# Low parts of two product tiles made by an accumulating DMA, in a cross-interaction tower kernel on one Trainium2 core

## The chip, the cores and the metric

The kernel runs on 1 of the 8 cores of a Trainium2 chip. The metric is the device time of one execution in microseconds (us). The engines are named as the profile does: PE (TensorE), PEld (its weight loads), DVE (VectorE), ACT (ScalarE), POOL (GpSimd) and SP (SyncE, which here only issues DMAs).

## What is computed

1024 rows of 32 table lookups (64 values each) give `e`, of shape (1024, 32, 64). Two interaction layers follow, then three small dense layers.

```python
def _cin_layer(h, h0, W, b):
    Wr = W.reshape(W.shape[0], h.shape[1], h0.shape[1])
    return jax.nn.relu(jnp.einsum('bhd,bmd,ohm->bod', h, h0, Wr) + b[None, :, None])
x1 = _cin_layer(e, e, W1, b1)              # W1: 128 x (32*32)
direct2 = _cin_layer(x1[:, :64], e, W2, b2)  # W2: 128 x (64*32)
z = jnp.sum(jnp.concatenate([x1[:, 64:], direct2], axis=1), axis=-1)
h = relu(concat([z, dense_ctx]) @ W_top1 + b_top1)
h = relu(h @ W_top2 + b_top2);  y = h @ W_top3
```

## The kernel before

The batch is cut into 128 chunks of 8 rows; 8 rows by 64 values are the 512 columns (`N`) of every matmul. A step of the pipeline is one chunk `c`; steps run in a loop unrolled six times, with the first six and the last eight written out. All engines run their own `step`, tied by semaphores that count chunks.

**Layer 1** of a chunk contracts products of `e` with itself. POOL forms four tiles of them (`prod1`, L258) from `near` and `h0`; a remainder of 32 rows (`rem_a` times `rem_b`, L245) is formed for two chunks at once, split into a high and a low part (ACT L618, L619; POOL L267), and contracted by one more matmul (L522). ACT turns the result into `x1` (L607), SP copies it to all partitions by DMA (`x1rep`, L311), and ACT moves that to PSUM (`x1p`, L638).

**Layer 2** contracts products of `x1` with `e`: 16 tiles of 128 x 512. DVE forms eight from `near` (`pnear`) and eight from `far` (`pfar`), both at L459. Twelve tiles (all of `pnear`, half of `pfar`) are split for fp32r: ACT rounds them to a high part `phi` (L655, L666), DVE subtracts to get the low part `plo` (L464), and PE does three fp32r matmuls on each (L527, L528 with `phi`, L533 with `plo`). The four tiles left stay fp32 (`whole`, L538); PE does each of these matmuls in two passes, so two entries stand in the trace for each.

The order in a step is written out for each engine:

- PE: high parts of `pnear` (16 matmuls), layer 1 of chunk c+2 (L521, L522), `whole`, low parts (12), high parts of `pfar` (8).
- DVE: `pnear`, `pfar`, low parts of `pnear` (L464, waits for `phi`), low parts of `pfar`.
- ACT: `x1` of chunk c+1, in even steps the remainder's high parts, `phi` of `pnear`, `x1p` of c+1, `phi` of `pfar`, sums of layer 2 of c-1 and of layer 1 of c+1 (L602, eight each).
- POOL: `prod1` of c+2; in odd steps `rem_prod`, in even steps the remainder's low part and the copy of indices (L232); two table gathers (L237), which end seven chunks before the end.
- SP: `x1rep` (waits for `x1`), in odd steps the remainder rows (L306), `near` and `h0` of c+3 (waits for `pnear`), `far` of c+2, in even steps the store of gathered rows (L318).

`prod1` is one buffer, so POOL waits before it for the layer-1 matmuls that read the last contents:

```python
                    pool.wait_ge(acc1_ready, c + 2)
```

Of the kernel before, what the change touches and what calls it, by code (L numbers as in the profile page):

```python
# [32 lines left out]

T_NEAR = A2 * K1
T_SPLIT = T_NEAR + K2
# [3 lines left out]
def build_dlrm(nc, a):  # L39
# [7 lines left out]
    with ctx:  # L47
# [23 lines left out]
        w2T = sb("w2T", [P, K2, O])  # L71
# [11 lines left out]
        prod1 = sb("prod1", [P, K1, N])  # L83
# [27 lines left out]
        w1wide = prod1[:, :, :].rearrange("o a n -> o (a n)")  # L111
# [4 lines left out]
        hid2 = [prod1[:, 2 * h:2 * h + 2, :] for h in range(2)]  # L116
# [38 lines left out]
        pfar_ready = sem("pfar_ready")  # L155
        hi_near_ready = sem("hi_near_ready")
# [64 lines left out]
        @block.gpsimd  # L221
        def _(pool):
            nc.gpsimd.memset(ident[:, :], 0.0).then_inc(ident_zero, 1)
            pool.wait_ge(ident_zero, 1)
            nc.gpsimd.affine_select(out=ident[:, :], in_=ident[:, :], compare_op=ALU.not_equal, fill=1.0,
                                    base=0, pattern=[[-1, P]], channel_multiplier=1).then_inc(ident_ready, 1)
            nc.gpsimd.memset(wt1a[0:H, :], 0.0)
            nc.gpsimd.memset(z1[0:H, :], 0.0).then_inc(top_zero, 1)
            pool.wait_ge(idx_all_ready, 1)

            def place_idx(pair, s):
                nc.gpsimd.tensor_copy(idx[s][:, :].unsqueeze(2), idx_all[:, :, bass.ds(pair, 1)]).then_inc(idx_ready, 1)  # L232
                pool.wait_ge(idx_ready, pair + 1)
                pool.sem_inc(lookups_begun, 1)

            def gather(g, s):
                nc.gpsimd.indirect_dma_start(  # L237
                    out=gathered[s][:, g, :], out_offset=None, in_=a["tables"],
                    in_offset=bass.IndirectOffsetOnAxis(ap=idx[s][:, g:g + 1], axis=0)).then_inc(rows_gathered[s], 16)

            def remainder_products(pair):
                pool.wait_ge(rem_in, 32 * pair + 32)

                pool.wait_ge(rem_lo_ready, pair)
                nc.gpsimd.tensor_tensor(rem_prod[:, :], rem_a[:, :], rem_b[:, :], ALU.mult).then_inc(rem_prod_ready, 1)  # L245

            for pair in range(3):
                place_idx(pair, pair)
                for g in range(PAIR_GATHERS):
                    gather(g, pair)  # L250

            def step(c, turn, u, at):
                pair, odd = turn * (U // 2) + u // 2, u % 2
                if within(at, 2):

                    pool.wait_ge(acc1_ready, c + 2)
# [24 lines left out]
        @block.sync
        def _(sp):
# [67 lines left out]
            def step(c, turn, u, at):  # L350
# [30 lines left out]
        def _(dve):  # L381
# [45 lines left out]
            dve.wait_ge(tp_filled, 3)  # L427
            nc.vector.tensor_copy(flat(w2T[:, :, :]), tp[0][:, :]).then_inc(tp_copied, 1)
            for h in range(T_SPLIT // K1):
                hi, lo = (flat(w[:, K1 * h:K1 * (h + 1), :]) for w in (w2hi, w2lo))  # L430
                dve.wait_ge(tp_filled, 4 + h)
                nc.vector.tensor_copy(hi, tp[1 - h % 2][:, :]).then_inc(part_hi, 1)
                dve.wait_ge(part_hi, h + 1)
                nc.vector.tensor_tensor(lo, tp[1 - h % 2][:, :], hi.bitcast(fp32), ALU.subtract).then_inc(tp_copied, 1)
# [19 lines left out]
            dve.wait_ge(acc1_ready, 1)  # L454
# [34 lines left out]
        def _(pe):  # L489
# [107 lines left out]
        def _(act):  # L597
# [45 lines left out]
            def step(c, turn, u, at):  # L643
# [11 lines left out]
                nc.scalar.copy(phi[:, 0:T_NEAR, :], pnear[:, :, :, :].rearrange("p a k n -> p (a k) n")).then_inc(hi_near_ready, 1)  # L655
# [10 lines left out]
                nc.scalar.copy(phi[:, T_NEAR:T_SPLIT, :], pfar[:, 0, :, :]).then_inc(hi_far_ready, 1)  # L666
# [43 lines left out]
```

## Time and profile before

| | |
|---|---|
| median of 3 runs | 2057.59 us (2054.43 to 2060.06) |
| the profiled execution | 2057.63 us |
| its span, first to last instruction | 2055.8 us |
| busy: PE, DVE | 2012.2 us (98%), 1983.9 us (96%) |
| busy: ACT, POOL | 1631.9 us (79%), 1524.0 us (74%) |
| 16 DMA engines, queue of SP | 66.7% busy, 397.10 MB |
| granted TensorE clock | 0.996 |

A busy share is time in instructions; matmuls overlap at their ends, so the step-to-step distance of an engine is read from starts in the timeline, not from durations. "Idle before, releaser" names what ended an engine's wait.

### The profile page before, as it was taken

To read this page: it belongs to the slowest core of one execution; us is meant where nothing else is said; L and a number is where in the kernel's file an instruction comes from. 1 tells how busy PE (TensorE), PEld (TensorE's weight loads), DVE (VectorE), ACT (ScalarE), POOL (GpSimd) and SP (SyncE) were. 2 spreads that over 40 slices of the span, in tenths; PEclk is the share of its full clock that TensorE was granted. 3 is DMA by queue.
4 is the path that set the end of the run, shared out by engine and by line. 5 is a ranking of instruction groups with operands and counts; after the bars stand their busy time and mean duration, and the time that the engine had idled before them with its cause. 6 is when DMAs were issued, how large, how long until landed. Compare 5 with 4: busy or idle time off the path is not lost.

```text
span 2055.8 us, 28705 instructions
## 1 busy us (share of the span) xinstructions
PE 2012.2 (98%) x6890; PEld 1299.2 (63%) x6890; DVE 1983.9 (96%) x545; ACT 1631.9 (79%) x4755; POOL 1524.0 (74%) x580
## 2 busy tenths in 40 slices
PE   3899999999999999999999999999999999999999
PEld 1566666666666666666666666666666666666664
DVE  5999999999999999999999999999999999999992
ACT  2788788788888888887887887887887888888873
POOL 3877787787787787787787788778778777778520
PEclk9999999999999999999999999999999999999999
DMA  6777777776776776776776776776777777767740
GB/s 185 215 210 208 198 213 203 198 217 199 200 214 200 204 215 196 207 216 190 211 213 195 208 216 192 210 212 191 215 208 197 211 205 201 212 200 206 210 108 1
DMA packets 239331, 406.51 MB, mean 198 GB/s; under 512 B 33377, under 2 KB 50273, under 8 KB 239090
## 3 DMA queue, kind: packets, MB, share of 16 engines
q1 hardware_dynamic: 231026, 397.10, 66.7%
q0 software_dynamic: 8192, 8.40, 2.0%
q14 instruction: 104, 0.85, 0.1%
q8 instruction: 9, 0.15, 0.0%
HBM read 321.49 MB, written 16.78 MB: 165 GB/s over the span
## 4 chain that ended last, share of the span: by engine, by line
DVE 59%; issue 35%; PE 3%; DMA 1%; SPq 1%; ACT 0%; DVEq 0%; POOL 0%; ACTq 0%; POOLq 0%
DVE pnear L459 27%; DVE pfar L459 16%; DVE plo L464 16%; PE acc L521 0%; ACT phi L655 0%; PE acc L527 0%; PE acc L538 0%; PE x1p L586 0%; PE acc L586 0%; PE acc L528 0%; DMA near<-emb_rows 0%; POOL gathered L237 0%; DMA rem_b<-emb_rows 0%; SPq L301 0%; PE acc L592 0%
## 5 line engine op out<-in xcount | busy, mean ns | idle before, releaser
L237 POOL DMA_INDIRECT gathered<-in_tables,idx x256 | 762.0, 2977 | 104.8 <-issue 52.8
L258 POOL TENSOR_TENSOR prod<-near,h 128x2048 f32<-128x2048 f32 x126 | 577.2, 4581 | 174.4 <-PE acc L522 168.7
L655 ACT CAST phi<-pnear 128x4096 fp32r<-128x4096 f32 x128 | 465.9, 3640 | 269.9 <-DVE pnear L459 269.9
L527 PE MATMUL acc<-phi,w2lo 128*128 128x512 f32 x1536 | 603.9, 393 | 14.3 <-ACT phi L655 14.3
L528 PE MATMUL acc<-phi,w2hi 128*128 128x512 f32 x1536 | 603.1, 393 | 0.0
L602 ACT ACTIVATE acc<-acc,bias 128x64 f32<-128x64 f32 (+1 forms) x2048 | 574.9, 283 | 11.7 <-PE acc L528 8.5
L464 DVE TENSOR_TENSOR plo<-pnear,phi 128x4096 fp32r<-128x4096 f32 x128 | 571.8, 4467 | 2.0 <-ACT phi L655 2.0
L459 DVE TENSOR_TENSOR pfar<-far,x1p 128x4096 f32<-128x4096 f32 x128 | 565.8, 4420 | 6.9 <-PE acc L538 1.1
L459 DVE TENSOR_TENSOR pnear<-near,x1p 128x4096 f32<-128x4096 f32 x128 | 564.9, 4414 | 4.7 <-ACT x1p L638 4.7
L521 PE MATMUL acc<-prod,w1T 128*128 128x512 f32 x1024 | 462.5, 594 | 14.3 <-DVE prod L444 12.9
L538 PE MATMUL acc<-pfar,w2T 128*128 128x512 f32 x1024 | 460.3, 592 | 0.0
L533 PE MATMUL acc<-plo,w2hi 128*128 128x512 f32 x1536 | 425.2, 426 | 0.0
L602 ACT ACTIVATION_READ_ACCUMULATOR acc<-acc,bias (+2 forms) x2048 | 420.9, 206 | 1.5
L533 PEld LDWEIGHTS acc<-plo,w2hi 128*128 128x128 f32 x1536 | 289.1, 188 | 115.6 <-issue 61.2
L527 PEld LDWEIGHTS acc<-phi,w2lo 128*128 128x128 f32 x1536 | 289.9, 189 | 79.7 <-ACT phi L655 16.3
L538 PEld LDWEIGHTS acc<-pfar,w2T 128*128 128x128 f32 x1024 | 194.1, 190 | 220.2 <-issue 214.5
L528 PEld LDWEIGHTS acc<-phi,w2hi 128*128 128x128 f32 x1536 | 289.8, 189 | 63.4
L521 PEld LDWEIGHTS acc<-prod,w1T 128*128 128x128 f32 x1024 | 194.3, 190 | 211.2 <-issue 198.2
L464 DVE TENSOR_TENSOR plo<-pfar,phi 128x2048 fp32r<-128x2048 f32 x128 | 293.4, 2292 | 0.0
L666 ACT CAST phi<-pfar 128x2048 fp32r<-128x2048 f32 x128 | 244.4, 1910 | 1.8 <-PE acc L528 0.9
L245 POOL TENSOR_TENSOR rem_prod<-rem_a,rem_b 32x512 f32<-32x512 f32 x63 | 81.6, 1294 | 150.1 <-DMA rem_b<-emb_rows 150.1
L607 ACT ACTIVATE x<-acc,bias 64x512 f32<-64x512 f32 x128 | 87.6, 684 | 84.5 <-PE acc L522 76.0
(68 smaller groups left out, 535.5 us busy)
## 6 DMA issues: line engine op xcount, KB each, us to landing
near<-emb_rows SPq DMA_DIRECT2D x512, 256.0 KB
far<-emb_rows SPq DMA_DIRECT2D x512, 256.0 KB, 4.2
x1rep<-x SPq DMA_DIRECT2D x256, 256.0 KB, 4.2
h<-emb_rows SPq DMA_DIRECT2D x128, 256.0 KB
emb_rows<-gathered SPq DMA_DIRECT2D x128, 128.0 KB, 3.5
gathered<-in_tables,idx POOLq DMA_INDIRECT x256, 4.9
rem_a<-emb_rows SPq DMA_DIRECT2D x64, 64.0 KB, 3.6
rem_b<-emb_rows SPq DMA_DIRECT2D x64, 64.0 KB, 3.0
```

The source lines that it names most:

```text
L237: nc.gpsimd.indirect_dma_start(out=gathered[s][:, g, :], out_offset=None, in_=a["tables"], in_offset=bass.IndirectOffsetOnAxis(ap=idx[s][: ...
L258: nc.gpsimd.tensor_tensor(prod1[:, :, :], near[(u + 2) % 3][:, :, :], h0[odd][:, :].unsqueeze(1).to_broadcast([P, K1, N]), ALU.mult).then_ ...
L459: return nc.vector.tensor_tensor(out, h0part.unsqueeze(1).to_broadcast([P, A2, k, N]), x1p[s][:, :].rearrange("p (a n) -> p a n", a=A2).un ...
L464: return nc.vector.tensor_tensor(plo[:, parts, :], whole.rearrange("p a k n -> p (a k) n"), phi[:, parts, :].bitcast(fp32), ALU.subtract)
L521: nc.tensor.matmul(acc1[s][:, :], w1T[:, k, :], prod1[:, k, :], start=(k == 0), stop=False)
L527: nc.tensor.matmul(acc2[s][:, :], w2lo[:, t, :], phi[:, t, :], start=(t == 0), stop=False)
L528: mm = nc.tensor.matmul(acc2[s][:, :], w2hi[:, t, :], phi[:, t, :], start=False, stop=(t == T_SPLIT - 1))
L533: mm = nc.tensor.matmul(acc2[s][:, :], w2hi[:, t, :], plo[:, t, :], start=False, stop=False)
L538: mm = nc.tensor.matmul(acc2[s][:, :], w2T[:, k, :], pfar[:, 1, k, :], start=False, stop=False)
L602: ins = nc.scalar.activation(acc[rows, cols], acc[rows, cols], ACT.Relu, bias=bias[rows, :], accum_out=z[rows, bass.ds(c * CB + b, 1)])
L655: nc.scalar.copy(phi[:, 0:T_NEAR, :], pnear[:, :, :, :].rearrange("p a k n -> p (a k) n")).then_inc(hi_near_ready, 1)
L666: nc.scalar.copy(phi[:, T_NEAR:T_SPLIT, :], pfar[:, 0, :, :]).then_inc(hi_far_ready, 1)
```

## The change

- `T_DMA = 2`: for the first two `pnear` tiles the low part is no longer made by DVE. ACT writes `phi` for them, then the negated products into `plo`, then `phi` for the other six tiles. POOL issues a DMA from `pnear` to `plo` that adds (`accum_op=ALU.add`). DVE's next `pnear` and PE's use of these two low parts wait for that DMA.
- `T_SPLIT` 12 to 13: one more `pfar` tile is split, three stay whole.
- `prod1` has two buffers, and POOL's wait before it is one chunk weaker.
- SP loads the remainder rows at the end of the even step, behind the store of gathered rows, for which it now waits; the store moves ahead of the `far` loads.

```diff
-T_SPLIT = T_NEAR + K2
+T_DMA = 2
+T_SPLIT = T_NEAR + K2 + 1
+T_WHOLE = T_NEAR + A2 * K2 - T_SPLIT
...
-        prod1 = sb("prod1", [P, K1, N])
+        prod1 = [sb(f"prod1_{s}", [P, K1, N]) for s in range(2)]
...
+            def low_parts(c):
+                pool.wait_ge(minus_ready, c + 1)
+                pool.sem_inc(lo_begun, 1)
+                nc.gpsimd.dma_start(plo[:, 0:T_DMA, :], pnear[:, 0, 0:T_DMA, :], accum_op=ALU.add
+                                    ).then_inc(lo_dma_in, 16)
...
-                    pool.wait_ge(acc1_ready, c + 2)
+                    pool.wait_ge(acc1_ready, c + 1 if begun(at) else 2)
...
+                low_parts(c)
                 if odd and within(at, 3):
                     remainder_products(pair + 2)
...
# SP
-                if odd and within(at, 3):
-                    sp.wait_ge(emb_stored, STORES * pair + 3 * STORES)
-                    sp.wait_ge(rem_prod_ready, pair + 2)
-                    load_rem((c + 3) * N)
...
+                if not odd and within(at, 5):
+                    store_rows(pair + 2, (u // 2 + 2) % 3, turn + (u // 2 + 2) // 3 + 1)
                 if within(at, 2):
                     sp.wait_ge(pfar_ready, c + 1)
                     load_far((c + 2) * N, odd)
                 if not odd and within(at, 5):
-                    store_rows(pair + 2, (u // 2 + 2) % 3, turn + (u // 2 + 2) // 3 + 1)
+                    sp.wait_ge(emb_stored, STORES * pair + 3 * STORES)
+                    sp.sem_inc(stores_begun, 1)
+                    sp.wait_ge(rem_prod_ready, pair + 2)
+                    load_rem((c + 4) * N)
...
# DVE
+                    dve.wait_ge(lo_dma_in, 16 * c)
                 products2(pnear[:, :, :, :], near[u % 3][:, :, :], odd, K1).then_inc(pnear_ready, 1)
...
-                low(slice(0, T_NEAR), pnear[:, :, :, :]).then_inc(lo_near_ready, 1)
+                low(slice(T_DMA, T_NEAR), pnear[:, :, :, :].rearrange("p a k n -> p (a k) n")[:, T_DMA:T_NEAR, :]).then_inc(lo_near_ready, 1)
...
# PE
-                pe.wait_ge(hi_near_ready, c + 1)
+                pe.wait_ge(hi_dma_ready, c + 1)
...
-                high(odd, range(0, T_NEAR)).then_inc(hi_near_used, 1)
+                high(odd, range(0, T_DMA))
+                pe.wait_ge(hi_near_ready, c + 1)
+                high(odd, range(T_DMA, T_NEAR)).then_inc(hi_near_used, 1)
...
+                pe.wait_ge(lo_dma_in, 16 * c + 16)
+                low(odd, range(0, T_DMA)).then_inc(lo_dma_used, 1)
                 pe.wait_ge(lo_near_ready, c + 1)
-                low(odd, range(0, T_NEAR))
+                low(odd, range(T_DMA, T_NEAR))
...
# ACT
-                nc.scalar.copy(phi[:, 0:T_NEAR, :], pnear[:, :, :, :].rearrange("p a k n -> p (a k) n")).then_inc(hi_near_ready, 1)
+                products = pnear[:, :, :, :].rearrange("p a k n -> p (a k) n")
+                nc.scalar.copy(phi[:, 0:T_DMA, :], products[:, 0:T_DMA, :]).then_inc(hi_dma_ready, 1)
+                if begun(at):
+                    act.wait_ge(lo_dma_used, c)
+                nc.scalar.activation(plo[:, 0:T_DMA, :], products[:, 0:T_DMA, :], ACT.Copy, scale=-1.0).then_inc(minus_ready, 1)
+                nc.scalar.copy(phi[:, T_DMA:T_NEAR, :], products[:, T_DMA:T_NEAR, :]).then_inc(hi_near_ready, 1)
```

ACT, an odd step without a remainder, before (first fence) and in the change (second). `products` of `pnear` come in, `phi` and `plo` go out:

```order
L607 ACTIVATE x<-acc_0,bias 64x512 [waits x1rep_in,acc1_ready]
L655 CAST phi<-pnear 128x4096 [waits hi_near_used,pnear_ready]
L638 COPY x1p<-x1rep 128x1024 [waits pfar_ready,x1rep_in]
L666 CAST phi<-pfar 128x2048 [waits acc2_ready,pfar_ready]
L602 ACTIVATE acc_0,z<-acc_0,bias 128x64 [waits acc2_ready]
L602 ACTIVATE acc_0,z<-acc_0,bias 128x64 x7
L602 ACTIVATE acc_0,z<-acc_0,bias 64x64 x8
```

```order
L632 ACTIVATE x<-acc_0,bias 64x512 [waits x1rep_in,acc1_ready]
L681 CAST phi<-pnear 128x1024 [waits hi_near_used,pnear_ready]
L684 ACTIVATE plo<-pnear 128x1024 [waits lo_dma_used]
L685 CAST phi<-pnear 128x3072
L663 COPY x1p<-x1rep 128x1024 [waits pfar_ready,x1rep_in]
L696 CAST phi<-pfar 128x2560 [waits acc2_ready,pfar_ready]
L627 ACTIVATE acc_0,z<-acc_0,bias 128x64 [waits acc2_ready]
L627 ACTIVATE acc_0,z<-acc_0,bias 128x64 x7
L627 ACTIVATE acc_0,z<-acc_0,bias 64x64 x8
```

One instruction became three ahead of `hi_near_ready`, which DVE's low parts wait for, and `phi` of `pfar` has 512 columns more.

POOL, the last gathers and all that follows them, before and in the change:

```order
L237 DMA gathered<-in_tables,idx 128x64 x2
L258 TENSOR_TENSOR prod<-near,h_0 128x2048 [waits near_in_1,acc1_ready]
L267 TENSOR_TENSOR rem_parts<-rem_prod,rem_parts 32x512 [waits p1_ready,rem_hi_ready]
L258 TENSOR_TENSOR prod<-near,h_1 128x2048 [waits near_in_2,acc1_ready,rem_lo_ready]
L245 TENSOR_TENSOR rem_prod<-rem_a,rem_b 32x512 [waits rem_lo_ready,rem_in]
L258 TENSOR_TENSOR prod<-near,h_0 128x2048 [waits near_in_0,acc1_ready]
L267 TENSOR_TENSOR rem_parts<-rem_prod,rem_parts 32x512 [waits p1_ready,rem_hi_ready]
L258 TENSOR_TENSOR prod<-near,h_1 128x2048 [waits near_in_1,acc1_ready,rem_lo_ready]
```

```order
L245 DMA gathered<-in_tables,idx 128x64 x2
L273 TENSOR_TENSOR prod_0<-near,h_0 128x2048 [waits near_in_1,acc1_ready]
L259 DMA plo<-pnear 128x1024 [waits minus_ready]
L283 TENSOR_TENSOR rem_parts<-rem_prod,rem_parts 32x512 [waits p1_ready,rem_hi_ready]
L273 TENSOR_TENSOR prod_1<-near,h_1 128x2048 [waits near_in_2,acc1_ready,rem_lo_ready]
L259 DMA plo<-pnear 128x1024 [waits minus_ready]
L253 TENSOR_TENSOR rem_prod<-rem_a,rem_b 32x512 [waits rem_lo_ready,rem_in]
L273 TENSOR_TENSOR prod_0<-near,h_0 128x2048 [waits near_in_0,acc1_ready]
L259 DMA plo<-pnear 128x1024 [waits minus_ready]
L283 TENSOR_TENSOR rem_parts<-rem_prod,rem_parts 32x512 [waits p1_ready,rem_hi_ready]
L273 TENSOR_TENSOR prod_1<-near,h_1 128x2048 [waits near_in_1,acc1_ready,rem_lo_ready]
```

The DMA issue stands between `prod` and the remainder's instruction of every step. The `acc1_ready` that `prod` waits for is now that of one chunk earlier, which the order cannot show.

## Rows read from the trace of the kernel before

**Rows 1.** PE busy, middle of the span (--windows; columns PE, PEld, DVE, ACT, POOL, clock, DMA).
```profile
200.00:1000.00 800.00, 800.00 (x2764) 520.55 (x2764) 797.32 (x209) 658.72 (x1937) 633.16 (x235) 1.00 0.72 206
```
**Rows 2.** PE and its weight loads, timeline, one step (start, duration).
```profile
1006.90 2.49 PEld L533 LDWEIGHTS acc<-plo,w2hi 128*128 128x128 f32 x11 [0.24 <-issue]
1009.65 0.39 PE L527 MATMUL acc<-phi,w2lo 128*128 128x512 f32 x1
1009.88 0.39 PE L528 MATMUL acc<-phi,w2hi 128*128 128x512 f32 x1
...
1015.58 0.19 PEld L521 LDWEIGHTS acc<-prod,w1T 128*128 128x128 f32 x1 [0.24 <-issue]
1016.01 0.19 PEld L521 LDWEIGHTS acc<-prod,w1T 128*128 128x128 f32 x1 [0.24 <-issue]
...
1025.01 0.39 PE L527 MATMUL acc<-phi,w2lo 128*128 128x512 f32 x1
```
**Rows 3.** DVE, timeline, one step.
```profile
1002.72 4.42 DVE L459 TENSOR_TENSOR pnear<-near,x1p 128x4096 f32<-128x4096 f32 x1
1007.19 4.42 DVE L459 TENSOR_TENSOR pfar<-far,x1p 128x4096 f32<-128x4096 f32 x1
1011.53 4.42 DVE L464 TENSOR_TENSOR plo<-pnear,phi 128x4096 fp32r<-128x4096 f32 x1
1015.87 2.29 DVE L464 TENSOR_TENSOR plo<-pfar,phi 128x2048 fp32r<-128x2048 f32 x1
1018.07 4.42 DVE L459 TENSOR_TENSOR pnear<-near,x1p 128x4096 f32<-128x4096 f32 x1
```
**Rows 4.** ACT, timeline, the same step (an even one, with remainder).
```profile
1004.33 0.60 ACT L618 CAST rem_parts<-rem_prod 32x512 fp32r<-32x512 f32 x1
1004.95 0.62 ACT L619 CAST rem_parts<-rem_prod 32x512 fp32r<-32x512 f32 x1
1007.16 3.65 ACT L655 CAST phi<-pnear 128x4096 fp32r<-128x4096 f32 x1 [1.60 <-DVE pnear L459]
1010.84 1.02 ACT L638 COPY x1p<-x1rep 128x1024 f32<-128x1024 f32 x1
1011.79 1.91 ACT L666 CAST phi<-pfar 128x2048 fp32r<-128x2048 f32 x1
1013.60 0.28 ACT L602 ACTIVATE acc<-acc,bias 128x64 f32<-128x64 f32 x1
```
**Rows 5.** POOL, timeline, the same step.
```profile
1008.36 1.30 POOL L267 TENSOR_TENSOR rem_parts<-rem_prod,rem_parts 32x512 fp32r<-32x512 f32 x1
1009.92 0.19 POOL L232 COPY idx<-idx_all 128x4 int32 x1 [0.26 <-POOL rem_parts L267]
1010.91 1.01 POOL L237 DMA_INDIRECT gathered<-in_tables,idx  x1 [0.81 <-POOL idx L232]
1012.22 4.55 POOL L237 DMA_INDIRECT gathered<-in_tables,idx  x1 [0.30 <-issue]
```
**Rows 6.** POOL and DVE, timeline, first step of the kernel.
```profile
52.91 4.53 POOL L258 TENSOR_TENSOR prod<-near,h 128x2048 f32<-128x2048 f32 x1 [2.40 <-DMA near<-emb_rows]
57.59 5.26 POOL L267 TENSOR_TENSOR rem_parts<-rem_prod,rem_parts 32x512 fp32r<-32x512 f32 x1
...
55.45 6.28 DVE L464 TENSOR_TENSOR plo<-pnear,phi 128x4096 fp32r<-128x4096 f32 x1 [2.03 <-ACT phi L655]
61.65 3.35 DVE L464 TENSOR_TENSOR plo<-pfar,phi 128x2048 fp32r<-128x2048 f32 x1
```
**Rows 7.** POOL, timeline, a prod near the end; SP, issue of near.
```profile
1955.87 4.58 POOL L258 TENSOR_TENSOR prod<-near,h 128x2048 f32<-128x2048 f32 x1 [7.54 <-PE acc L522]
...
1007.96 2.74 SPq L296 DMA_DIRECT2D near<-emb_rows  x4
```
**Rows 8.** DMA issues of the whole span (KB each, median us to landing).
```profile
far<-emb_rows SPq DMA_DIRECT2D x512, 256.0 KB, 4.2
gathered<-in_tables,idx POOLq DMA_INDIRECT x256, 4.9
```
**Rows 9.** The last DVE instruction, timeline, and PE's last matmul on phi (--tile, first and last start).
```profile
2013.93 2.29 DVE L464 TENSOR_TENSOR plo<-pfar,phi 128x2048 fp32r<-128x2048 f32 x1
...
L528 PE MATMUL acc<-phi,w2hi x1536: 388/392/628, 56.1 to 2022.2; 128*128 128x512 f32 x192
```

More of the change, by code:

```diff
@@ L110, in build_dlrm @@
         w2n = far[1][:, :, :].rearrange("o a n -> o (a n)")
-        w1wide = prod1[:, :, :].rearrange("o a n -> o (a n)")
+        w1wide = prod1[0][:, :, :].rearrange("o a n -> o (a n)")
         w2wide = pnear[:, :, :, :].rearrange("o a k n -> o (a k n)")
@@ L115, in build_dlrm @@
         hid1 = [pnear[:, 0, :, :], pnear[:, 1, :, :]]
-        hid2 = [prod1[:, 2 * h:2 * h + 2, :] for h in range(2)]
+        hid2 = [prod1[0][:, 2 * h:2 * h + 2, :] for h in range(2)]
         w1_in = sem("w1_in")
@@ L155, in build_dlrm @@
         pfar_ready = sem("pfar_ready")
+        hi_dma_ready = sem("hi_dma_ready")
+        minus_ready = sem("minus_ready")
+        lo_begun = sem("lo_begun")
+        lo_dma_in = sem("lo_dma_in")
+        lo_dma_used = sem("lo_dma_used")
         hi_near_ready = sem("hi_near_ready")
@@ L426, in _ @@
             nc.vector.tensor_copy(flat(w1remT[:, :, :]), tp[1][0:3 * REM, 0:2 * P]).then_inc(tp_copied, 1)
[L427 to L434, printed above, removed]
+            T_FAR = T_NEAR + K2
+            for n, tiles in enumerate((range(T_FAR, T_SPLIT), range(0, K1), range(K1, T_NEAR), range(T_NEAR, T_FAR))):
+                turned = tp[n % 2][:, 0:len(tiles) * O]
+                dve.wait_ge(tp_filled, 3 + n)
+                if n == 0:
+                    last = nc.vector.tensor_copy(flat(w2T[:, :, :]), tp[0][:, len(tiles) * O:K2 * O])
+                if tiles:
+                    hi, lo = (flat(w[:, tiles.start:tiles.stop, :]) for w in (w2hi, w2lo))
+                    nc.vector.tensor_copy(hi, turned).then_inc(part_hi, 1)
+                    dve.wait_ge(part_hi, n + 1)
+                    last = nc.vector.tensor_tensor(lo, turned, hi.bitcast(fp32), ALU.subtract)
+                last.then_inc(tp_copied, 1)
             dve.wait_ge(top_zero, 1)
@@ L443, in products1 @@
                 dve.wait_ge(near_in[s], LOADS)
-                nc.vector.tensor_tensor(prod1[:, :, :], near[s][:, :, :],
+                nc.vector.tensor_tensor(prod1[s][:, :, :], near[s][:, :, :],
                                         h0[s][:, :].unsqueeze(1).to_broadcast([P, K1, N]), ALU.mult).then_inc(p1_ready, 1)
@@ L463, in low @@
             def low(parts, whole):
-                return nc.vector.tensor_tensor(plo[:, parts, :], whole.rearrange("p a k n -> p (a k) n"),
+                return nc.vector.tensor_tensor(plo[:, parts, :], whole,
                                                phi[:, parts, :].bitcast(fp32), ALU.subtract)
@@ L481, in step @@
                     dve.wait_ge(lo_used, c)
-                low(slice(0, T_NEAR), pnear[:, :, :, :]).then_inc(lo_near_ready, 1)
+                low(slice(T_DMA, T_NEAR), pnear[:, :, :, :].rearrange("p a k n -> p (a k) n")[:, T_DMA:T_NEAR, :]).then_inc(lo_near_ready, 1)
                 dve.wait_ge(hi_far_ready, c + 1)
-                low(slice(T_NEAR, T_SPLIT), pfar[:, 0:1, :, :]).then_inc(lo_far_ready, 1)
+                low(slice(T_NEAR, T_SPLIT), pfar[:, :, :, :].rearrange("p a k n -> p (a k) n")[:, 0:T_SPLIT - T_NEAR, :]).then_inc(lo_far_ready, 1)
             software_pipeline(dve, step)
@@ L520, in layer1 @@
                 for k in range(K1):
-                    nc.tensor.matmul(acc1[s][:, :], w1T[:, k, :], prod1[:, k, :], start=(k == 0), stop=False)
+                    nc.tensor.matmul(acc1[s][:, :], w1T[:, k, :], prod1[s][:, k, :], start=(k == 0), stop=False)
                 nc.tensor.matmul(acc1[s][:, :], w1remT[:, s, :], rem_parts[:, :],
@@ L536, in whole @@
             def whole(s):
-                for k in range(K2):
-                    mm = nc.tensor.matmul(acc2[s][:, :], w2T[:, k, :], pfar[:, 1, k, :], start=False, stop=False)
+                for k in range(T_WHOLE):
+                    mm = nc.tensor.matmul(acc2[s][:, :], w2T[:, k, :], pfar[:, 1, K2 - T_WHOLE + k, :], start=False, stop=False)
                 return mm
@@ L665, in step @@
                     act.wait_ge(acc2_ready, c)
-                nc.scalar.copy(phi[:, T_NEAR:T_SPLIT, :], pfar[:, 0, :, :]).then_inc(hi_far_ready, 1)
+                nc.scalar.copy(phi[:, T_NEAR:T_SPLIT, :], pfar[:, :, :, :].rearrange("p a k n -> p (a k) n")[:, 0:T_SPLIT - T_NEAR, :]).then_inc(hi_far_ready, 1)
                 if begun(at):
```

5 lines of the change are left out of this document (2 added, 3 removed).

## The prediction

> **What bounds the kernel now.** I read the busy time by stretches first. In the middle PE is busy 800.00 of 800.00 us, but DVE is busy 797.32 [rows 1], so neither share decides; the step has to be summed for each. In PE's timeline one step lasts from 1009.65 to 1025.01, 15.36 us [rows 2]. Its distances are 0.229 us for an fp32r matmul on `phi` (1009.65 to 1009.88), 0.43 us for a pass of an fp32 matmul (1015.58 to 1016.01) and 0.23 us for one on `plo` (eleven in 2.49). Summed: 24 x 0.229 + 16 x 0.43 + one remainder matmul 0.23 + 12 x 0.23 = 5.50 + 6.88 + 0.23 + 2.76 = 15.37. That is the measured step: PE never waits and sets it. DVE's own distances are 4.34 us from `pfar` to the low part (1007.19 to 1011.53), 4.34 for the low part of eight tiles, 2.20 for that of four [rows 3]. `pnear` to `pfar` would be 4.34 as well, but is 4.47: the wait on `whole`. DVE alone would need 4.34 + 4.34 + 4.34 + 2.20 = 15.22, only 0.14 less than PE. So two engines are near the bound, and what both wait for matters more than either sum.
>
> **PE's part of the change.** One tile leaves `whole` (2 x 0.43) and comes to the split ones (2 x 0.229 + 0.23). Saved: 0.86 - 0.69 = 0.17 us a step. The new PE step is 15.19. Over some 125 steps this is 21 us, the most that the change can bring in the steady part. Work on PE that starts as two tiles, then six, adds nothing.
>
> **DVE's part.** The low part of `pnear` has six tiles, that of `pfar` five. Between the distances of four and eight tiles [rows 3], six are 3.27 and five are 2.74. DVE's own work falls to 4.34 + 4.34 + 3.27 + 2.74 = 14.69, and 0.5 us a step would be free.
>
> **ACT, which stands between the two.** DVE's low part needs `hi_near_ready`. Before, ACT starts 0.02 us after `pnear` ends (1002.72 + 4.42 to 1007.16) and is done at 1010.81 [rows 3, 4], while DVE is in `pfar` until 1011.53: 0.7 us in hand. Now three instructions stand there. From 3.65 us for 4096 columns and 1.91 for 2048 [rows 4] a column costs 0.85 ns and an instruction 0.18 us, so 1024 columns take 1.04 and 3072 take 2.78. I take the negated one, which is nearest to a copy of its size, at 1.04 too; the 1024-column copy to PSUM took 1.02. With 0.03 from one to the next (1010.81 to 1010.84) the six tiles are ready 0.02 + 1.04 + 0.03 + 1.04 + 0.03 + 2.78 = 4.94 us after `pnear` ends, and DVE, free at 4.34 less 0.08 of overlap, waits 0.6 us or more. This is a loop through one step: 4.42 (`pnear`) + 4.94 + 3.27 + 2.74 = 15.37. The `pfar` branch of ACT is as tight: after 4.94 come `x1p`, 0.03 + 0.95 to the next start [rows 4], then 2560 columns, 2.34, so `hi_far_ready` is at 8.26, where DVE arrives at 4.94 + 3.27 = 8.21. By this branch the step is 4.42 + 8.26 + 2.74 = 15.42. Instead of DVE's 14.69 or PE's 15.19 I expect 15.40, between the two branches, 0.04 above now: 125 x 0.04 = **+5 us**. ACT as a whole has room: it adds 1.04 + 1.04 + 2.78 - 3.65 + 0.43 = 1.6 us to a step, and its waits for `pnear` alone are 1.60 us in the even step [rows 4] with the remainder. PE's matmuls on `phi` keep up.
>
> The Trainium skill (Perfetto Trace Analysis, Optimizing Scalar/DVE Operations) says that part of a ScalarE instruction's profiled latency, the acknowledged write, overlaps with the next. By it four handoffs would shrink by 0.09 each and the step would fall under PE's 15.19. The two remainder casts, SBUF to SBUF, do not overlap (1004.33 + 0.60, next at 1004.95), while ACT before a read of PSUM does, by 0.10 (1013.70 to 1013.60) [rows 4]; so the row next of kin says no, and the page makes a rival.
>
> **POOL's part.** The issue of the adding DMA has no row. Lower bound: an undisturbed gather issue, 1.01 us; upper: one that met a low part, 4.55 [rows 5]. I take 1.01, nearest in kind (128 descriptors of an undisturbed issue). The negated part is ready at 0.02 + 1.04 + 0.03 + 1.04 = 2.13 after `pnear` ends; with gaps of 0.15 and 0.10 the issue ends at 3.29 and the remainder's instruction (1.30) at 4.69. DVE's low part starts at 4.94. That order counts: in the first step `prod` was running when the low part started at 55.45, and this took 6.28 instead of 4.42, that is until 4.42 after `prod` ended at 57.44; then `rem_parts`, queued during the low part, went ahead of the next one, which took 3.35 instead of 2.29 [rows 6]. A POOL instruction that reads SBUF and a DVE one with two SBUF operands exclude each other, and one of POOL that queues is served before DVE's next. The Trainium skill (SBUF — State Buffer, Who interferes with whom) has the same exclusion; it infers that writing descriptors is not held up by such a DVE instruction, which no row here shows. The copy of indices (0.19, some 0.2 behind the remainder, even steps only) [rows 5] comes out at 4.9, on the edge; half of 62 steps x 0.2 = **+6 us**. The gathers queue behind the low parts as before, and cost DVE nothing. `prod` then starts when the second low part is over, beside `pnear`.
>
> **The end.** Once gathers stop, nothing holds `prod` back: its wait for `acc1_ready`, 7.54 us before the change [rows 7], is one chunk weaker. In three steps (prod of chunks 125 to 127) it starts when `near` has landed. The last `near` DMA is issued about 1010.1, 3.0 after `pnear`'s end, and with the 4.2 of `far` [rows 7, 8] lands at 7.2: within the first low part (4.94 to 8.21). So `prod` goes ahead of the second low part and delays it by its 4.58 us: 3 x 4.5 = **+14 us**.
> Behind DVE's last instruction PE had 6.0 us until its last start (2016.2 to 2022.2) [rows 9], a backlog that a waiting PE has not: 5 x 0.23 + 9 x 0.229 = 3.2. **-3 us.**
>
> **At nothing:** SP. `far` is issued 1.5 us later in even steps and has a step to land; the remainder rows now come a step before `rem_prod`, so POOL's wait for them goes; it was beside DVE's `pfar`, and gives nothing to DVE or PE. The wait for the store holds SP until some 8.5 us after `pnear`; the next `x1rep` is at 13. The second `prod1` buffer saves a wait in the prologue that `pnear` does not need. The adding DMA is issued at 3.3 and the next `pnear` starts at 11: 7.7 us for it, where far takes 4.2 and a gather 4.9 [rows 8] to land.
>
> **Sum:** against the profiled execution's 2057.6 (the median is 2057.59): 2057.6 + 5 + 6 + 14 - 3 = 2079.6; I say **2079**. Its own range is 2062 (no index term, `near` landing after the low part) to 2095.
>
> **Rivals.**
> *A: PE is the bound, faster.* If ACT's handoffs overlap by 0.1 each, the loop is below 15.19 and PE's 0.17 comes in: 2057.6 - 21 = 2036; with the delay at the end, of which DVE's free 0.5 us a step takes back some, 2036 + 12 = 2048. For it: overlap is seen at PSUM reads. Against: the two casts. Takes 2033 to 2051. Chance 0.25.
> *B: POOL's remainder instruction runs into DVE's low part, slower.* Point of decision: an issue longer than 1.25 us (4.94 - 4.69 + 1.01). Beyond it each 0.1 us costs 0.1 a step, 12 us in all, up to 1.3 x 125 = 160. An issue of 1.6 gives 2079 + 44 = 2123, of 2.0 gives 2173, at most 2235. For it: the DMA reads its destination too, more descriptors than a gather. Chance 0.24.
> *C: the adding DMA is late.* It moves 512 KB and reads 512 KB more, amid `near` and `far` (DMA 72% busy [rows 1]). If it takes longer than 7.7 us, `pnear` waits: 1 us late is 125 us. Against: all landings in rows 8 are under 5. 2100 to 2250, chance 0.08.
> *D: no change*: ACT slightly quicker and no collision at the end, 2052 to 2063. Chance 0.08.
>
> **The numbers.** The forecast has 0.35. About 0.3% (6 us) is what a measurement can tell. Faster: A, 0.25, and 0.01 of D. Same: most of D and the forecast's low edge, 0.12. Slower: 0.62. The range is 2037 to 2165: it leaves out A's lower end (0.05), B beyond an issue of 1.9 us (0.08) and the worse half of C (0.05), together under 0.2.
>
> **What would show it.** In the profile after: DVE's wait "plo <- ACT phi", 0.6 us in nearly every step (125 x 0.6 = 75 us); steps of 15.40; PE with some waits for `phi`; the POOL issue at 1.0 us; L484 undisturbed at 3.35 and 2.82 in the middle; three second low parts near 7.3 us at the end. PE without waits and a step of 15.19 prove A; L484 stretched in most steps proves B; DVE `pnear` waiting for a DMA proves C.

## The result, and the profile after

| | before | after |
|---|---|---|
| median | 2058.19 us (4 runs, 2054.43 to 2060.06) | 2074.18 us (4 runs, 2073.2 to 2075.0) |
| profiled execution, its span | 2057.63, 2055.8 us | 2074.93, 2073.1 us |
| 16 DMA engines, POOL's queue | 2.0% busy, 8.40 MB | 19.5% busy, 75.52 MB |

The ratio is 1.0083, with a 95% interval of 1.0069 to 1.0097: slower by 16 us, well beyond 0.3%. 2079 had been forecast. But the 16 us are not the sum that I made.

The page of the kernel after: busy times, POOL's queue, and groups of instructions.

```profile
PE 2006.5 (97%) x7018; PEld 1312.5 (63%) x7018; DVE 1930.8 (93%) x547; ACT 1820.5 (88%) x5011; POOL 1698.3 (82%) x708
...
q0 software_dynamic: 26624, 75.52, 19.5%
...
L484 DVE TENSOR_TENSOR plo<-pnear,phi 128x3072 fp32r<-128x3072 f32 x128 | 449.3, 3510 | 77.1 <-ACT phi L685 77.1
...
L259 POOL DMA_DIRECT2D plo<-pnear x128 | 126.4, 988 | 157.9 <-ACT plo L684 146.8
```

The stretch of [rows 1], same columns (PE, PEld, DVE, ACT, POOL, clock, DMA share, GB/s), after:

```profile
200.00:1000.00 800.00, 789.15 (x2779) 518.90 (x2777) 768.20 (x207) 727.98 (x2024) 696.65 (x284) 1.00 0.87 237
```

PE and DVE were busy for all but 3 of 800 us [rows 1]; now PE lacks 11 and DVE 32. So neither is the bound. ACT has gained 69 us, and the DMA engines are 87% busy instead of 72%.

**The steady step** of the kernel after, in the timeline: DVE's rows, which answer to [rows 3], then ACT's to [rows 4], then POOL's to [rows 5].

```profile
1012.30 4.41 DVE L479 TENSOR_TENSOR pnear<-near,x1p 128x4096 f32<-128x4096 f32 x1
1016.63 4.41 DVE L479 TENSOR_TENSOR pfar<-far,x1p 128x4096 f32<-128x4096 f32 x1
1021.44 3.48 DVE L484 TENSOR_TENSOR plo<-pnear,phi 128x3072 fp32r<-128x3072 f32 x1 [0.41 <-ACT phi L685]
1024.85 2.81 DVE L484 TENSOR_TENSOR plo<-pfar,phi 128x2560 fp32r<-128x2560 f32 x1
1027.58 4.41 DVE L479 TENSOR_TENSOR pnear<-near,x1p 128x4096 f32<-128x4096 f32 x1
...
1016.74 1.06 ACT L681 CAST phi<-pnear 128x1024 fp32r<-128x1024 f32 x1 [0.50 <-DVE pnear L479]
1017.70 1.05 ACT L684 ACTIVATE plo<-pnear 128x1024 fp32r<-128x1024 f32 x1
1018.65 2.75 ACT L685 CAST phi<-pnear 128x3072 fp32r<-128x3072 f32 x1
...
1019.35 0.99 POOL L259 DMA_DIRECT2D plo<-pnear  x1 [1.49 <-ACT plo L684]
1020.41 1.30 POOL L283 TENSOR_TENSOR rem_parts<-rem_prod,rem_parts 32x512 fp32r<-32x512 f32 x1
```

From `pnear` to `pnear` it is 15.28 us: 4.33 + 4.81 (4.40 and the wait of 0.41) + 3.41 + 2.73. That is 0.07 less than before, not 0.04 more. Two things are to be seen. Two of ACT's instructions start before the end of the one ahead of them: 1016.74 + 1.06 is 1017.80, and the next starts at 1017.70. And POOL's instruction on the remainder starts at 1020.41 and still runs when the low part starts at 1021.44, which then takes 3.48.

**Where the 19 us are.** Since every step has one `pnear`, the distances of its starts cut the whole run into steps. Of the last `pnear`'s delay, 2019.8 against 2000.9, this is the division:

| | median step | beyond it, at 18 turns of the loop | beyond it, in the other steps | first, last `pnear` |
|---|---|---|---|---|
| before | 15.35 | -0.5 | 1.1 | 44.7, 2000.9 |
| after | 15.28 | 22.4 | 5.5 | 45.2, 2019.8 |

The first two distances, in which the pipeline fills, are left out of the last but one column: they stand 6.1 us above the median in both kernels. The steady part brings 127 x 0.07 = 9 us. The turns of the loop, one in every six steps, take 23, the other irregular steps 4 to 5. What comes behind the last `pnear` is 1.6 us shorter (53.3 against 54.9).

A turn, in the timeline of the kernel after, ACT and then DVE:

```profile
891.85 0.69 ACT L632 ACTIVATE x<-acc,bias 64x512 f32<-64x512 f32 x1 [1.71 <-issue]
892.43 0.60 ACT L643 CAST rem_parts<-rem_prod 32x512 fp32r<-32x512 f32 x1
893.05 0.62 ACT L644 CAST rem_parts<-rem_prod 32x512 fp32r<-32x512 f32 x1
893.70 1.06 ACT L681 CAST phi<-pnear 128x1024 fp32r<-128x1024 f32 x1
...
888.06 4.41 DVE L479 TENSOR_TENSOR pnear<-near,x1p 128x4096 f32<-128x4096 f32 x1
892.39 4.41 DVE L479 TENSOR_TENSOR pfar<-far,x1p 128x4096 f32<-128x4096 f32 x1
898.39 3.45 DVE L484 TENSOR_TENSOR plo<-pnear,phi 128x3072 fp32r<-128x3072 f32 x1 [1.59 <-ACT phi L685]
```

At the loop's jump ACT waits 1.71 us for nothing but its own next instruction ("issue"). Then four instructions stand back to back and the cast of `phi` comes 1.23 us behind `pnear`'s end (888.06 + 4.41 = 892.47). Before the change ACT idled 1.60 us at this place in an even step [rows 4]; now it idles 0.50. The wait for the code no longer fits in, and DVE waits 1.18 us longer than its 0.41. The waits of the kernel after (us in total, times, longest):

```profile
ACT x L632 <- issue: 32.9, 18, 2.2
DVE plo L484 <- ACT phi L685: 77.1, 128, 2.8
```

Before there were 7.9 us in 6 such waits of ACT, the longest 1.5.

### The profile page after: what moved, and what is told of

Same layout as the page of the kernel before. It is cut to its first block, busy times and chain, and to the rows that moved or that the text cites. A ratio compares the mean times of both kernels' runs of the same rounds, so it can differ in the third digit from the quotient of the medians.

```text
span 2073.1 us, 29734 instructions
## 1 busy us (share of the span) xinstructions
PE 2006.5 (97%) x7018; PEld 1312.5 (63%) x7018; DVE 1930.8 (93%) x547; ACT 1820.5 (88%) x5011; POOL 1698.3 (82%) x708
## 3 DMA queue, kind: packets, MB, share of 16 engines
q0 software_dynamic: 26624, 75.52, 19.5%
## 4 chain that ended last, share of the span: by engine, by line
DVE 39%; ACT 28%; issue 21%; DMA 5%; PE 2%; POOL 2%; SPq 1%; ACTq 0%; DVEq 0%; POOLq 0%
DVE pnear L479 23%; DVE plo L484 17%; ACT phi L685 14%; ACT plo L684 6%; ACT acc L627 4%; DMA plo<-pnear 3%; ACT phi L696 2%; ACT phi L681 1%; POOL prod L273 1%; DMA near<-emb_rows 1%; POOL gathered L245 1%; POOL idx L240 1%; ACT rem_parts L644 1%; PE acc L611 0%; PE x1p L611 0%
## 5 line engine op out<-in xcount | busy, mean ns | idle before, releaser
L245 POOL DMA_INDIRECT gathered<-in_tables,idx x256 | 629.9, 2460 | 102.1 <-POOL idx L240 52.4
L548 PE MATMUL acc<-phi,w2lo 128*128 128x512 f32 x1664 | 664.2, 399 | 40.5 <-ACT phi L685 28.4
L549 PE MATMUL acc<-phi,w2hi 128*128 128x512 f32 x1664 | 654.1, 393 | 0.0
L484 DVE TENSOR_TENSOR plo<-pnear,phi 128x3072 fp32r<-128x3072 f32 x128 | 449.3, 3510 | 77.1 <-ACT phi L685 77.1
L484 DVE TENSOR_TENSOR plo<-pfar,phi 128x2560 fp32r<-128x2560 f32 x128 | 360.8, 2818 | 0.1
L685 ACT CAST phi<-pnear 128x3072 fp32r<-128x3072 f32 x128 | 352.3, 2752 | 0.0
L559 PE MATMUL acc<-pfar,w2T 128*128 128x512 f32 x768 | 350.6, 592 | 0.0
L696 ACT CAST phi<-pfar 128x2560 fp32r<-128x2560 f32 x128 | 299.4, 2339 | 0.0
L259 POOL DMA_DIRECT2D plo<-pnear x128 | 126.4, 988 | 157.9 <-ACT plo L684 146.8
L681 ACT CAST phi<-pnear 128x1024 fp32r<-128x1024 f32 x128 | 135.0, 1055 | 136.8 <-DVE pnear L479 136.3
```

Source lines behind the costliest of these rows:

```text
L245: nc.gpsimd.indirect_dma_start(out=gathered[s][:, g, :], out_offset=None, in_=a["tables"], in_offset=bass.IndirectOffsetOnAxis(ap=idx[s][: ...
L484: return nc.vector.tensor_tensor(plo[:, parts, :], whole, phi[:, parts, :].bitcast(fp32), ALU.subtract)
L548: nc.tensor.matmul(acc2[s][:, :], w2lo[:, t, :], phi[:, t, :], start=(t == 0), stop=False)
L549: mm = nc.tensor.matmul(acc2[s][:, :], w2hi[:, t, :], phi[:, t, :], start=False, stop=(t == T_SPLIT - 1))
L685: nc.scalar.copy(phi[:, T_DMA:T_NEAR, :], products[:, T_DMA:T_NEAR, :]).then_inc(hi_near_ready, 1)
L696: nc.scalar.copy(phi[:, T_NEAR:T_SPLIT, :], pfar[:, :, :, :].rearrange("p a k n -> p (a k) n")[:, 0:T_SPLIT - T_NEAR, :]).then_inc(hi_far_ ...
```

## The experiments

**Is it the jump?** The long steps come every six, as the turns do, but the tables' data or the even steps could do that too. First the loop's window was moved by one step, so that a turn begins with an odd step:

```diff
-            for c in range(U):
+            for c in range(U + 1):
...
-                for u in range(U):
+                for u in range(1, U + 1):
```

> The changed kernel with the loop's window moved by one step, so that its jump stands ahead of an odd step (no remainder on ScalarE) instead of an even one. Theory J (ScalarE pays about 2.1 us for each of the 19 jumps, and in even steps only 0.5 us of slack hides it): the slack ahead of an odd step is 1.6 us, so each long step falls from 16.3-16.9 to under 16 and the time to 2074 - 19 x 1.1 = about 2053 us. Rival K (the long steps come from data movement or from GpSimd, once in six steps by the pattern of gathers and stores): no change, 2074 us within 3.

Measured: 2084.21 us, ratio 1.013 (1.0113 to 1.0146). The long steps moved with the turn, from steps 12, 18, 24 to 13, 19, 25, so neither data nor parity makes them. But they became dearer, most of them 17.0 to 17.6 us where they were 16.1 to 17.0. One turn of that run, ACT's timeline:

```profile
912.51 0.69 ACT L632 ACTIVATE x<-acc,bias 64x512 f32<-64x512 f32 x1 [2.31 <-issue]
914.38 1.05 ACT L681 CAST phi<-pnear 128x1024 fp32r<-128x1024 f32 x1 [1.18 <-issue]
```

There are two gaps now, of 2.31 and 1.18 us. The forecast for this run, 2053 us, was 31 us off: my argument that an odd step would have room for the gap was wrong, as the gap itself depends on where the jump lies. Why was not settled.

**Fewer jumps.** The loop's body was made twelve steps long in place of six (11 fewer turns):

```diff
-U = 6
+U = 12
```

> The changed kernel with the loop unrolled twelve times instead of six: 8 jumps instead of 19. Theory J: 11 jumps fewer at 1.3 us each, 2074 - 14 = 2060 us. Rival K (once in six steps by the data's pattern, not by the jump): 2074 us, with long steps still every sixth.

Measured: 2063.35 us, ratio 1.0028 (1.0018 to 1.0037), 10.8 us under the change. The long steps stand every twelve. The same with 30 steps, on both kernels:

> The kernel before with the loop unrolled thirty times. Its ScalarE has 1.6 to 2.7 us of slack in each step, and the wait for instructions behind a jump shows in 6 of 19 only. Theory J: the jumps are hidden, 2057 us, at most 2 us less. If a jump costs the same in any kernel: 17 x 1.3 = 22 us less, 2036 us.

> The changed kernel with the loop unrolled thirty times and nothing else. Theory J: 17 jumps fewer at 1.0 to 1.3 us (the twelvefold loop gave 11 us for 11 jumps), so 2074 - 17 to 22 = 2052 to 2057 us, and steps of 15.28 between. Rival (the jumps only take the place of waits that come up elsewhere, as in rem_first_u30): 2065 us or more.

Before with 30: 2059.71, ratio 1.0011 (1.0002 to 1.002), nothing gained: before the change the jumps are hidden in ACT's idle time. After with 30: 2060.67, ratio 1.0014 (1.0004 to 1.0024), 13.5 us less than with six. These two share a length of body and differ by 1 us: the jumps are most of what the change costs, 13.5 of the 16 us. The expectation was some 5 us too low; single steps of 15.6 to 16.9 us stay, and one of 18.8, which is the one turn that is left (ACT waits 3.5 us there).

**Without the adding DMA.** POOL still waits for the negated parts, but only raises the semaphore; the sum for two tiles is left out:

```diff
-                nc.gpsimd.dma_start(plo[:, 0:T_DMA, :], pnear[:, 0, 0:T_DMA, :], accum_op=ALU.add
-                                    ).then_inc(lo_dma_in, 16)
+                pool.sem_inc(lo_dma_in, 16)
```

> The changed kernel without the adding DMA: GpSimd still waits for the negated parts, and raises the semaphore itself. The low parts of two tiles are then wrong; what is left out is the adding DMA with its issue. Theory J: the DMA is not on the path of a step, so the steps stay 15.28 us, the long ones stay, and the time is 2069 to 2075 us (the issue of 1.0 us on GpSimd goes as well, which takes away the small overlap of the remainder's instruction with the low part, 0.12 us a step at most). Rival D (the 67 MB more of DMA traffic cost the time): back to 2058 or less, and no long steps.

Measured: 2050.14 us, ratio 0.9962 (0.9948 to 0.9976): 24 us less than the change, and far from what I expected. Waits and one group of that run:

```profile
ACT x L631 <- issue: 20.6, 18, 1.3
...
DVE plo L483 <- ACT phi L684: 61.9, 117, 2.8
```

```profile
L483 DVE TENSOR_TENSOR plo<-pnear,phi 128x3072 fp32r<-128x3072 f32 x128 | 431.8, 3374 | 62.3 <-ACT phi L684 61.9
```

Three things go with the DMA. ACT's wait at a jump is 1.14 us (20.6 / 18) instead of 1.83 (32.9 / 18), so the turns cost 12.5 us beyond the median step in place of 22.4. The low part takes 3.37 us instead of 3.51, as POOL's remainder instruction is done before it; the step is 15.21, which is 9 us over the run. The irregular steps are gone (5.5 to 0.0). The issue and the traffic are left out together here, so this run does not tell them apart. With 2.4 at the first `pnear` these make 26.7, and the last `pnear` starts 26.5 us earlier. The DMA of 512 KB a step thus costs 24 us with its issue, though DVE waits for its data only three times, 3.0 us in all.

**One tile by the DMA instead of two** (half the traffic, shorter ACT work):

```diff
-T_DMA = 2
+T_DMA = 1
```

> T_DMA = 1: one low part by DMA instead of two. ScalarE's chain ahead of the low parts falls by about 0.85 us and VectorE has 0.55 us more of its own work, so VectorE needs 15.22 us a step without waiting and TensorE 15.19. Theory J: the steps are 15.22 instead of 15.28 (-7 us) and ScalarE's slack in an even step rises by 0.8 us, so the jumps cost 19 x 0.8 less (-15 us): about 2052 us. Rival (two low parts by DMA are what makes the time; with one VectorE is the bound and more of it is lost to GpSimd): 2074 us or more.

Measured: 2068.13, ratio 1.0051 (1.0034 to 1.0068). The turns cost 2.4 us, but steps alternate between 15.27 and 15.69: DVE's low part of seven tiles starts earlier, right into POOL's instruction. So the time is 16 us above the 2052 expected. ACT's waits at the jumps:

```profile
ACT x L632 <- issue: 20.8, 18, 1.3
```

That is 1.16 us each, as without any adding DMA (1.14), though the DMA engines were 80% busy in the stretch of [rows 1] and not 72%. So the wait does not grow in proportion to the busy share. With the whole DMA of 512 KB it is 1.83 here (87%) and 1.5 to 2.0 in two runs below.

**The remainder's instruction ahead of the adding DMA** on POOL, so that it ends before the low part starts:

```diff
-                low_parts(c)
                 if odd and within(at, 3):
...
                     pool.wait_ge(rem_lo_ready, pair + 2)
+                low_parts(c)
                 if within(at, 7 - odd):
```

> The changed kernel with GpSimd's order turned in each step: the remainder's instruction first, then the wait for the negated parts and the issue of the adding DMA. Theory P (in the changed kernel the 1.0 us issue pushes the remainder's instruction 0.25 us into the low part of pnear, which takes 3.475 instead of 3.36 us and costs 0.07 us a step, as the run without the DMA shows): the low part is back at 3.36, the steps are 15.21 instead of 15.28, and the time is 2074 - 9 = 2065 us; the jumps stay. Rival D (the step is longer through the DMA traffic, not through GpSimd's order): steps of 15.28 and 2074 us.

Measured: 2078.6, ratio 1.0097 (1.0083 to 1.0112). The low part takes 3.36 and the median step is 15.21, as expected, so POOL's order is what had cost the 0.07 us a step. But the time is 14 us above the 2065 expected: the turns cost 27.9 us (ACT's wait there is 36.4 / 18 = 2.02) and the irregular steps 10. Of these 10, 6.4 are DVE's waits for the adding DMA itself, in 11 steps; the twelfth and longest, 4.6 us, is in the very first step, while the pipeline fills:

```profile
DVE pnear L479 <- DMA plo<-pnear: 11.0, 12, 4.6
```

Another kind occurs once. It is shown in ACT's and DVE's timeline:

```profile
1007.98 1.02 ACT L663 COPY x1p<-x1rep 128x1024 f32<-128x1024 f32 x1 [0.78 <-DMA x1rep<-x]
...
1011.30 2.83 DVE L484 TENSOR_TENSOR plo<-pfar,phi 128x2560 fp32r<-128x2560 f32 x1 [0.70 <-ACT phi L696]
```

Here a DMA of SP is late, and ACT's cast behind it holds DVE. Why the adding DMA is late more often in this order was not settled. The same order with a body of 30 steps:

> rem_first with the loop unrolled thirty times: one or two jumps instead of 19. Theory J (each jump costs 1.3 us since ScalarE waits about 1.8 us for its instructions there and has 0.5 us of slack): 17 x 1.3 = 22 us below rem_first, 2043 us, which is below the kernel before. If jumps and the order are not what costs, no difference from rem_first.

Measured: 2064.35, ratio 1.0033 (1.0022 to 1.0045), with single times from 2056 to 2070. That is 14 us less than with six, but 21 above the expectation, which left the late DMAs out: DVE waits 15.0 us for the adding DMA here, in 18 places.

**Both together**, one tile and the remainder first, with a body of six and of 30:

> One low part by DMA, remainder's instruction first, loop unrolled six times as in the change. Theory: the order alone takes the stretched low parts away (steps of 15.27), and since ScalarE has 0.85 us more slack the jumps cost some 0.3 us each: 2050 + 5 = 2055 us. If the jumps cost 1.3 us here too: 2072 us.

> The same with one low part by DMA instead of two. VectorE's own work is then 4.33 + 4.33 + 3.80 + 2.73 = 15.19 us a step and ScalarE has 0.85 us more slack. Theory P + J: steps of 15.20, no stretched low parts, 2040 to 2045 us, like rem_first_u30 with two. If the alternation 15.27 / 15.69 of one_tile stays, GpSimd's remainder instruction is not what stretched its low parts, and the time is 2060 us.

Measured: 2052.94, ratio 0.9981 (0.9972 to 0.9991), and 2049.98, ratio 0.9961 (0.9948 to 0.9973). The expectation for the first (2055) was near, that for the second (2040 to 2045) too low. The second is the fastest that computes everything, and 0.4% under the kernel before. A step with six, DVE's timeline, and the stretch of [rows 1]:

```profile
1001.82 4.41 DVE L479 TENSOR_TENSOR pnear<-near,x1p 128x4096 f32<-128x4096 f32 x1
1006.15 4.41 DVE L479 TENSOR_TENSOR pfar<-far,x1p 128x4096 f32<-128x4096 f32 x1
1010.54 3.89 DVE L484 TENSOR_TENSOR plo<-pnear,phi 128x3584 fp32r<-128x3584 f32 x1
1014.35 2.82 DVE L484 TENSOR_TENSOR plo<-pfar,phi 128x2560 fp32r<-128x2560 f32 x1
1017.09 4.41 DVE L479 TENSOR_TENSOR pnear<-near,x1p 128x4096 f32<-128x4096 f32 x1
```

```profile
200.00:1000.00 800.00, 799.45 (x2825) 528.17 (x2824) 797.95 (x210) 714.86 (x2040) 694.82 (x287) 1.00 0.80 224
```

DVE waits for nothing in this step, it is 15.27 long, and the DMA share is 80%. Both engines are full, as before the change, with 0.08 us less in a step: 10 us over the run, of which 4 to 8 come out.

**ACT makes `phi` of six tiles before the negated parts**, so that DVE need not wait:

```diff
                 nc.scalar.copy(phi[:, 0:T_DMA, :], products[:, 0:T_DMA, :]).then_inc(hi_dma_ready, 1)
+                nc.scalar.copy(phi[:, T_DMA:T_NEAR, :], products[:, T_DMA:T_NEAR, :]).then_inc(hi_near_ready, 1)
...
-                nc.scalar.copy(phi[:, T_DMA:T_NEAR, :], products[:, T_DMA:T_NEAR, :]).then_inc(hi_near_ready, 1)
```

> The changed kernel with ScalarE's high parts of the six tiles ahead of the negated parts. VectorE's wait for phi (0.41 us a step) must vanish, as the high parts come 0.96 us earlier; but the negated parts and the adding DMA come 2.75 us later. Theory D2 (the adding DMA takes 6 to 8.5 us under the loads and is nearly late already: the last full step waited 1.13 us for it): VectorE's next pnear waits for it, steps of 16 us or more, about 2074 + 125 x 1 = 2200 us. Rival (the DMA has much time in hand): steps of 15.20 by TensorE and about 2060 us.

Measured: 2273.23, ratio 1.1054 (1.1033 to 1.1075). Here rival C's mechanism can be seen, the adding DMA that comes late. DVE and POOL in the timeline of this run:

```profile
1013.14 3.35 DVE L484 TENSOR_TENSOR plo<-pnear,phi 128x3072 fp32r<-128x3072 f32 x1
...
1014.21 0.99 POOL L259 DMA_DIRECT2D plo<-pnear  x1 [4.43 <-ACT plo L685]
...
1021.14 4.42 DVE L479 TENSOR_TENSOR pnear<-near,x1p 128x4096 f32<-128x4096 f32 x1 [0.84 <-DMA plo<-pnear]
```

From the start of the issue to the end of the wait are 6.93 us (median of all landings 7.1, longest 9.0); DVE's waits for this DMA sum to 148.7 us. That is not all of the 199 us above the change: POOL's remainder instruction comes later too and runs into the low part of `pfar`, which takes 3.35 us in the median instead of 2.81. In the change as it is the issue starts 8.2 us ahead of the next `pnear` (1019.35 to 1027.58), so by these landings the DMA has about 1 us in hand.

**The rest of the change alone**: no part by DMA and 12 split tiles, as before, but two `prod1` buffers and the remainder rows in the even step.

```diff
-T_DMA = 2
-T_SPLIT = T_NEAR + K2 + 1
+T_DMA = 0
+T_SPLIT = T_NEAR + K2
...
-                low_parts(c)
```

> The rest of the change alone: no low part by DMA, twelve tiles split as before, but two prod1 buffers, and the remainder rows loaded in the even step. The forecast put this part at nothing, except for prod running into the second low part at the end, 14 us. Theory: TensorE sets the steps at 15.36, 2058 us within 3. Rival (GpSimd's prod, no longer held back, meets VectorE's low parts): up to 4.5 us in steps where it does, 2070 us or more.

Measured: 2566.98, ratio 1.2498 (1.2465 to 1.2532). POOL and DVE in its timeline:

```profile
1010.65 5.98 POOL L273 TENSOR_TENSOR prod<-near,h 128x2048 f32<-128x2048 f32 x1 [7.87 <-DMA near<-emb_rows]
...
1012.17 6.60 DVE L483 TENSOR_TENSOR plo<-pfar,phi 128x2048 fp32r<-128x2048 f32 x1
1018.70 4.41 DVE L478 TENSOR_TENSOR pnear<-near,x1p 128x4096 f32<-128x4096 f32 x1
```

`prod`, which no longer waits for PE, is queued while the first low part runs and goes ahead of the second, which takes 6.60 instead of 2.29 [rows 3]. That is 4.31 us in each step, 19.53 in place of 15.36 in all. PE was busy 857 us between 500 and 1500 us, and the granted clock there was 0.94. So one buffer was no shortage but an order: the wait for PE kept `prod` beside `pnear`. (The new place of the remainder rows is in this run too and was not tried by itself; but what releases `prod` in the trace is the landing of `near`, where before it was PE.) In the change POOL's wait for the negated part keeps `prod` out of the low parts' way: the run without the adding DMA has two buffers and this wait, and its steps are 15.21.

## Why the prediction was right, and where it was wrong

The side, the size (2079 against 2074) and the range were right, and so was the bound: DVE waits for ACT's `phi` in every step, and PE's 0.17 us does not come in. That the size came out is luck, as the terms show. So is the sum of these waits, 77.1 us where 75 was forecast: the steady wait is 0.41 us and not 0.6, which makes some 47 us with the first steps, and 30 come from the 18 turns, which the forecast did not have. The sum, term by term:

- **"With 0.03 from one to the next"** was wrong. `pnear`'s end to the low part is 4.73 us and not 4.94: two overlaps of 0.10 stand in place of two gaps of 0.03, and small differences in the other distances take back 0.05. I weighed rows of two casts on 32 partitions, SBUF to SBUF, against rows of a read of PSUM, and took the first as next of kin. The Trainium skill (Perfetto Trace Analysis, Optimizing Scalar/DVE Operations) says that the end of a ScalarE instruction overlaps with the next one; the trace agrees here, by 0.10 (1016.74 + 1.06 against 1017.70). Instead of 15.40 the step is 15.28, and 15.21 where nothing of POOL is in the way. The term was +5 and is -9. Rival A's condition held, with less than half of its gain: by the loop from ACT to DVE the step is 4.34 + 4.82 + 3.32 + 2.74 = 15.22 in the run without the DMA, not under PE's 15.19.
- **The index copy, +6**, is nothing: it comes half a us into DVE's low part (at 1021.97) and is held up itself, 3.00 us. In its place stands rival B in small. The issue took 0.99 us, as taken (1.01), but ACT's overlap let DVE's low part start while POOL's remainder instruction still ran. That costs 0.07 us a step, 9 in all. Where DVE starts sooner still (one tile), it costs 0.42 in every other step.
- **The end, +14**, failed in its landing time. POOL and DVE of the kernel after:

```profile
1959.67 4.62 POOL L273 TENSOR_TENSOR prod<-near,h 128x2048 f32<-128x2048 f32 x1 [7.78 <-DMA near<-emb_rows]
...
1946.82 4.41 DVE L479 TENSOR_TENSOR pfar<-far,x1p 128x4096 f32<-128x4096 f32 x1
...
1958.98 4.42 DVE L479 TENSOR_TENSOR pnear<-near,x1p 128x4096 f32<-128x4096 f32 x1 [1.13 <-DMA plo<-pnear]
```

`near` landed 12.8 us behind `pnear`'s end (1942.49 + 4.41 to 1959.67), not 7.2, so `prod` came after both low parts and met none. I had counted the last issue and the landing of `far` alone. The adding DMA has a share in that: in the run without it a `near` at this place landed 9.3 us behind `pnear`'s end (1917.22 + 4.41 to 1930.88), also too late to hold up DVE; and in the middle of the run of the rest alone 7.1 us, as forecast (999.17 + 4.41 to 1010.65). The collision as a mechanism is right, 4.31 us where 4.5 was put, as the run of the rest alone shows. What the end does cost is 1.1 us, once, for an adding DMA that was 9.4 us from the start of its issue (1949.54) to the end of DVE's wait. **PE's backlog, -3,** was -1.6.
- **"ACT as a whole has room"** is the step that failed most. It was said of a whole step, and by the prediction's own numbers, 1.6 us more work against 1.60 idle, the even step had next to none. ACT's idle time in an even step fell from 1.60 to 0.50 us, and at each turn of the loop ACT needs some 1.8 for its instructions. That is 23 us in all; no term stood for it.
- **The DMA engines** were looked at for rival C alone, the landing of the adding DMA. It mostly landed in time: 5.9 us from the end of its issue in the run shown above (6.93 - 0.99), where 7.7 were given. But without it the wait at the jump is 0.7 us shorter, and the irregular steps are gone.
- **The second buffer, "at nothing"**, held, but only with POOL's new wait in front of the remainder; without that wait and the rest of the DMA part the time is some 500 us longer.

So the total came near through opposite errors. Against the sum of 2079.6 stand -14 in the step (POOL's 9 in it), -6 at the index copy, -14 at the end, +1 behind it, +23 at the jumps and +4 in irregular steps (the 1.1 at the end in it): 2074.

Left open: why the moved window made the turns dearer, and which transfer delays which in the irregular steps. Four of these (about 1 us each, some 26 steps apart) have POOL's issue about 1.0 us late for no releaser that shows. What that does is plain: POOL's remainder instruction is late too, and the low part of `pnear` takes 4.4 us instead of 3.5. Where the delay comes from is not shown.

## What to carry to other kernels

Read an engine's slack where it is smallest, in the step with the most work and at a loop's jump, not from its busy share: a wait for code is free only as long as something else is waited for there. Work that is moved to a DMA is not paid for at its landing alone, but also in what its issue and its traffic do to other work, here the wait at a jump above all. And before a buffer is doubled, ask what order the single one had been keeping.

## What the runs showed of the hardware

A jump of a loop costs ACT a wait that is longer beside the large adding DMA: 1.14 us on average without it (DMA engines 72% busy), 1.16 with half of it (80%), 1.83 with all of it (87%). The Trainium skill (Runtime: NRT & Kernel Launch, Instruction fetch mechanics) says that a taken branch outside the loaded window forces a DMA fetch of the target before execution goes on. The trace agrees in so far as the waits stand only at turns, and longer bodies make them fewer; no row shows the fetch itself, nor how the traffic would hold it up. A POOL instruction that reads SBUF and is queued while a DVE instruction with two SBUF operands runs is served before DVE's next one of that kind, and cost it 4.31 us in every step. DVE's `pnear`, which reads `x1p` from PSUM, took its 4.41 us beside `prod` (1012.30 beside 1013.23 in the change). The issue of the adding DMA was not held up either: in the run with the six tiles first it took 0.99 us in the middle of such a low part (1014.21 within 1013.14 to 1016.49), and neither was longer for it. The Trainium skill (SBUF — State Buffer, Who interferes with whom) had inferred this; no row before the change showed it. It does not carry over to the indirect gathers here: in the change their issue took 0.98 us beside `pnear` (at 1028.90), but 2.83 where it met a low part (at 1025.78).
